# A deformable and a dynamic depthwise convolution: the chain of y in four steps, lag 19, taps two to a product, biases in one turn, pads ahead of the pivot

## The chip, the cores and the metric

The kernel runs on one core of one Trainium2 chip. The metric is the device time of one execution in microseconds; the median of the runs is given.

## The reference, cut to what matters

The input x is (8, 32, 192, 192) in fp32. Two stages, each preceded by a group norm of 16 groups of two channels, and each added to its input:

```python
def _L0(x, w_off, b_off, w_dcn, b_dcn):          # x: normalized
    off = (sigmoid(conv2d(x, w_off, b_off, 1)) - 0.5) * 2.0     # 3x3, 32 -> 64: dx, dy in (-1, 1)
    ix, iy = reflect(column - dx), reflect(row - dy)
    sampled = bilinear(x, iy, ix)                # per pixel and channel
    return conv2d(sampled, w_dcn, b_dcn, 1)      # 3x3, 32 -> 32

def _L1(y, w1, b1, w2, b2):                      # y: normalized
    hdn = relu(y.mean(axis=(2, 3)) @ w1 + b1)    # 64 per image
    kernels = (hdn @ w2 + b2).reshape(b, 32, 3, 3)
    return depthwise_conv3x3(y, kernels)         # own taps for each image and channel

y = x + _L0(group_norm(x), ...)
return y + _L1(group_norm(y), ...)
```

The taps of the second stage depend on the mean and the variance of the whole image y, so no row of the output can be made before the last row of y is there.

## The kernel before, in words

**Tiling.** An image is 12 chunks of 16 rows (CHUNKS), spread over 128 partitions; B = 8 images make TOTAL = 96 chunks. One loop of steps i runs on each engine, each writes its own order by hand, and semaphores tie them together; b, o = divmod(i, 12). In step i the engines work on these chunks:

- Chunk i: TensorE (PE) makes the offset convolution into the bank pair z (offsets, L357). ScalarE (ACT) takes its tanh, sign and size (offset, side, size) and copies neighbours (sides). VectorE (DVE) mixes the samples (sample, L699 to L727), nine instructions, the last at L727.
- Chunk i - 3 (DCN_STEP): PE's deformable convolution into dc in two halves (deform, L397 to L406). DVE adds bias and residual (evacuate, L739) and so has y in the ring yr of YS = 15 chunks; ACT sums its squares (y_square).
- Chunk i - 17 (DW_STEP): PE's depthwise convolution in two halves (depthwise, L427), into the one bank dw, each half emptied by ACT (finish, L575). For the last image the two banks dc are free and are used in turn. Steps 99 to 112 hold only this work.

PE's order in a step: offsets, first half of depthwise, first half of deform, second half of depthwise, second half of deform.

**Small work once an image.** All small products write columns of one bank sm and take turns in the order of small_order: PE waits until ACT has read the result before (small_turn). For the norm of y of image b - 1: y_totals on ACT at o = 3, y_means on PE at the end of o = 3, ACT reads it at o = 4, POOL computes the norm (y_norm, L856 to L868) and writes pads (set_y_pads), PE makes the hidden layer (hidden, L476) behind the offset products of o = 4 and the 16 taps (taps, L483) behind the first half of deform of the same step. In fp32 each product is two instructions. ACT reads the taps at o = 5, POOL makes the depthwise weights wy (y_weights) and PE their bias (y_bias, L493) at o = 5, where the depthwise of the image begins.

For the norm of the next x: SP loads its eight plane tiles at o = 0 to 7 (st_load), ACT sums each a step later (x_sums, L583 and L586), shifted by a pivot value, which POOL takes from the first tile (pivot, L770, at o = 0). x_mean, x_var and x_biases follow on PE at the ends of o = 9, 10 and 11. x_biases makes two groups of bias products (L444, L464) with a read of ACT between them.

**Pads.** set_pads(n) (L824, L830) writes the halo columns of chunk n's input, which PE's offset products and ACT's sides wait for. For the first chunk of an image it runs at o = 11 of the image before, behind x_weights; for the second and third at o = 0 behind pivot. set_s_pads, set_first_edge and set_last_edge do the same for the sampled rows. set_y_edges (POOL, four small DMAs at o = 4, two images later) writes the last row's halo in y.

**SP.** In step i it issues the store of chunk i - 18, the shifts of sampled rows (s_shift, behind sampled), the loads of chunk i + 2 (x_load), a plane tile, the residual rows of chunk i - 3, and the shift of y rows for chunk i - 15 (y_shift; for the first of an image i - 16, which waits for the pads of y).

Of the kernel before, what the change touches and what calls it, by code (L numbers as in the profile page):

```python
# [30 lines left out]
XS, SS, YS, HS = 3, 3, 15, 4  # L31
# [15 lines left out]
DW_STEP = 17  # L47
# [50 lines left out]
def small_order():  # L98

    order = [("xm", 0), ("xv", 0), ("ob", 0), ("db", 0)]  # L100
    for b in range(B + 1):
        if b:
            order += [("ym", b - 1), ("hid", b - 1), ("tap", b - 1), ("wb", b - 1)]
        if b + 1 < B:
            order += [("xm", b + 1), ("xv", b + 1), ("ob", b + 1), ("db", b + 1)]
    return {key: i for i, key in enumerate(order)}
# [5 lines left out]
def block_kernel(nc, x, planes, w_off, b_off, w_dcn, b_dcn, w1, b1, w2, b2, consts, xr, out):  # L112
    with ExitStack() as ctx:
# [17 lines left out]
        ypad = sb("ypad", [P, Q, PW])  # L131
# [9 lines left out]
        w1r = sb("w1r", [P, Q, HID])  # L141
        w2r = sb("w2r", [HID, TAPS, P])
        b2r = sb("b2r", [P, TAPS])
        b1c = sb("b1c", [HID, 1])
# [22 lines left out]
        hid = sb("hid", [HID, 1])  # L167
# [183 lines left out]
        def _(pe):  # L351
# [87 lines left out]
            def biases(what, b, col, sets, mean):  # L439
                small_turn(what, b)  # L440
                for at, weights in enumerate(sets):
                    for kx in range(3):
                        for m in halves:
                            last = nc.tensor.matmul(sm[m, col + at:col + at + 1], weights[:, kx, :], mean,  # L444
                                                    start=kx == 0, stop=kx == 2)
                last.then_inc(small, 1)

# [8 lines left out]
            def x_biases(b):  # L456
                pe.wait_ge(wo_ok, b + 1)
                biases("ob", b, C_OB, (wos[b % 2][:, 0], wos[b % 2][:, 1]), nmx[b % 2][:])
                pe.wait_ge(wd_ok, b + 1)
                small_turn("db", b)  # L460
                for q in range(Q):
                    for kx in range(3):
                        for g in range(G):
                            last = nc.tensor.matmul(sm[C * g:C * g + C, C_DB + q:C_DB + q + 1], wds[b % 2][:, kx, q],  # L464
                                                    nmx[b % 2][:], start=kx == 0, stop=kx == 2)
# [6 lines left out]
            def hidden(b):  # L472
                pe.wait_ge(y_step, Y_STEPS * b + 7)
                small_turn("hid", b)
                for q in range(Q):
                    last = nc.tensor.matmul(sm[0:HID, C_HID:C_HID + 1], w1r[:, q], pooled[:, q:q + 1],  # L476
# [3 lines left out]
            def taps(b):  # L480
                small_turn("tap", b)
                for t in range(TAPS):
                    last = nc.tensor.matmul(sm[:, C_TAP + t:C_TAP + t + 1], w2r[:, t, :], hid[:],  # L483
                                            start=True, stop=True)
# [17 lines left out]
            for i in range(STEPS):  # L502
# [5 lines left out]
                if 0 < b <= B and o == 4:  # L508
                    hidden(b - 1)
                if 0 < b <= B and o == 5:  # L510
# [5 lines left out]
                if 0 < b <= B and o == 4:  # L516
# [5 lines left out]
                if 0 < b <= B and o == 3:  # L522
                    y_means(b - 1)
                if b + 1 < B:
# [8 lines left out]
        def _(act):  # L533
# [86 lines left out]

            def off_bias(b):
# [4 lines left out]
                                     bias=bo[:, 1:2], scale=0.5).then_inc(small_rd, 1)  # L626
                act.wait_ge(small_rd, SMALL["ob", b] + 1)
                act.wait_ge(small, SMALL["db", b] + 1)
                nc.scalar.activation(db[b % 2][:, 0:1], sm[:, C_DB:C_DB + 1], ACT.Identity, bias=bd[:, 0:1])
                nc.scalar.activation(db[b % 2][:, 1:2], sm[:, C_DB + 1:C_DB + 2], ACT.Identity,  # L630
                                     bias=bd[:, 1:2]).then_inc(small_rd, 1)
# [17 lines left out]
            for i in range(STEPS):  # L649
# [8 lines left out]
                if 0 < b <= B and o == 5:  # L658
                    read("tap", b - 1, tapr[:], sm[:, C_TAP:C_TAP + TAPS])
# [18 lines left out]
                if 0 < b <= B and o == 4:  # L678
                    read("hid", b - 1, hid[:], sm[0:HID, C_HID:C_HID + 1], ACT.Relu, bias=b1c[:], scale=1.0 / (2 * G))
                if 0 < b <= B and o == 5:  # L680
# [10 lines left out]
        def _(dve):  # L691
# [38 lines left out]
            def evacuate(n):  # L730
# [3 lines left out]
                if j == 0:  # L734
                    dve.wait_ge(small_rd, SMALL["db", b] + 1)
# [8 lines left out]
            dve.wait_ge(cleared, 3)  # L744
# [16 lines left out]
        def _(pool):  # L761
# [83 lines left out]
            def set_last_edge(b):  # L845
                q = slice(P // 2, P)
                pool.wait_ge(dcn_mm, 2 * (CHUNKS * b + CHUNKS - SS))
                if b + 1 < B:
                    pool.wait_ge(pads, pads_set(CHUNKS * (b + 1)))
# [20 lines left out]
            def set_y_pads(b):  # L870
# [8 lines left out]
                wait(pool, e_in, 16 * EDGES * b)  # L879
# [140 lines left out]
```

## Time and profile before

| | |
|---|---|
| median of 3 runs | 1694.75 us (1694.44 to 1696.19) |
| profiled execution | 1700.7 us, its span 1698.9 us |
| PE busy | 1574.7 us, 93% |
| DVE busy | 1356.8 us, 80% |
| ACT busy | 1052.9 us, 62% |
| POOL busy | 313.5 us, 18% |
| mean granted clock of PE | 0.967 |
| hardware DMA queue | 304 MB, 60.5% of 16 engines |

All times of the trace are microseconds from the start of the span. A busy PE is not a PE at its peak: records of products overlap. The granted clock is the share of PE's full rate (1.00 is 2.4 GHz, 0.50 is 1.2). "Idle before" and the bracket behind an instruction say how long its engine did nothing and what ended that.

### The profile page before, as it was taken

The numbers are of one execution on the slowest core, as the hardware profiler recorded it, in microseconds if no ns is written. First come the engines' busy times: TensorE is split into PE (matmuls) and PEld (weight loads), VectorE is DVE, ScalarE is ACT, GpSimd is POOL, SyncE is SP. The second block draws the span as 40 slices with busy tenths as digits, with TensorE's granted clock in tenths as the row PEclk, the third lists the DMA queues.
The fourth block names the chain that finished last, engine by engine and source line by source line (L and its number), as shares of the span: only waits on it lengthen the run. The fifth ranks groups of instructions, "written<-read, shape, count | busy, mean of one in ns | idle before, by whom it ended". The sixth has DMA issues, their size and how long they took to land.

```text
span 1698.9 us, 30216 instructions
## 1 busy us (share of the span) xinstructions
PE 1574.7 (93%) x12176; PEld 671.1 (40%) x12176; DVE 1356.8 (80%) x1264; ACT 1052.9 (62%) x1586; POOL 313.5 (18%) x381
## 2 busy tenths in 40 slices
PE   3779878999999999999999999999999999999887
PEld 1333334333443334433443334433444334533343
DVE  3899989798879978799887987798787898889700
ACT  4766556765777566666667656676575765655413
POOL 3000312012230221203230122301403031300010
PEclk9899999999999999999999999999999999999979
DMA  7355446666666665666666666666565765556436
GB/s 231 107 178 169 140 124 198 174 200 202 191 210 196 173 205 169 193 203 195 184 207 184 199 198 179 194 197 191 168 213 171 220 171 164 177 158 193 132 89 199
DMA packets 225195, 307.73 MB, mean 181 GB/s; under 512 B 16656, under 2 KB 167552, under 8 KB 224992
## 3 DMA queue, kind: packets, MB, share of 16 engines
q1 hardware_dynamic: 223632, 304.42, 60.5%
q8 instruction: 96, 1.57, 0.4%
q0 software_dynamic: 1424, 1.38, 0.3%
q14 instruction: 43, 0.35, 0.1%
HBM read 190.11 MB, written 38.14 MB: 134 GB/s over the span
## 4 chain that ended last, share of the span: by engine, by line
PE 54%; DVE 19%; ACT 11%; issue 6%; DMA 5%; POOL 3%; SPq 2%; DVEq 0%; ACTq 0%; POOLq 0%
PE z L357 25%; PE dc L397 13%; PE dw L427 9%; DMA st<-in_planes 4%; DVE nb L718 3%; DVE nb L713 3%; DVE nb L716 3%; PE sm L483 2%; ACT dv L540 2%; PE dc L427 2%; DVE xv L706 2%; DVE nb L720 2%; DVE nb L722 2%; ACT mv L547 2%; DVE nb L707 2%
## 5 line engine op out<-in xcount | busy, mean ns | idle before, releaser
L357 PE MATMUL z<-xv,wos 128*64 128x384 f32 x4608 | 775.5, 493 | 33.9 <-issue 22.6
L357 PEld LDWEIGHTS z<-xv,wos 128*64 128x64 f32 x4608 | 333.6, 137 | 454.0 <-issue 445.8
L397 PE MATMUL dc<-sr,wds 128*32 128x384 f32 x2304 | 453.4, 525 | 25.7 <-DVE yr L739 25.6
L397 PE MATMUL dc<-sh,wds 128*32 128x384 f32 x2112 | 411.8, 527 | 0.0
L699 DVE COPY_PREDICATED nb<-mu,xv 128x2280 f32<-128x2280 uint16 x96 | 268.8, 2800 | 100.0 <-ACT mu L547 99.1
L427 PE MATMUL dw<-yr,wy 128*64 128x388 f32 x672 | 258.1, 506 | 4.6 <-ACT ot L575 3.7
L427 PE MATMUL dw<-yh,wy 128*64 128x388 f32 x672 | 258.2, 506 | 0.0
L540 ACT ACTIVATE du<-z,ob 128x768 f32<-128x768 f32 x96 | 86.3, 899 | 275.2 <-PE z L357 275.2
L397 PEld LDWEIGHTS dc<-sr,wds 128*32 128x32 f32 x2304 | 123.4, 111 | 296.4 <-issue 294.8
L561 ACT ACTIVATE nb<-xv 128x2292 f32<-128x2292 f32 x96 | 202.7, 2112 | 41.7 <-issue 41.3
L706 DVE COPY_PREDICATED xv<-mv,xv 128x768 f32<-128x768 uint16 x96 | 102.5, 1067 | 90.6 <-ACT mv L547 67.7
L718 DVE TENSOR_TENSOR nb<-nb,xv 128x1536 f32<-128x1536 f32 x96 | 169.6, 1767 | 3.3
L716 DVE TENSOR_TENSOR nb<-nb,du 128x1536 f32<-128x1536 f32 x96 | 169.0, 1760 | 3.3
L713 DVE TENSOR_TENSOR nb<-nb,xv 128x1536 f32<-128x1536 f32 x96 | 169.0, 1760 | 3.3
L427 PEld LDWEIGHTS dw<-yr,wy 128*64 128x64 f32 x672 | 84.1, 137 | 139.9 <-issue 87.2
L575 ACT ACTIVATE ot<-dw,wb 128x388 f32<-128x388 f32 x168 | 96.7, 576 | 68.8 <-PE dw L427 68.4
L594 ACT ACTIVATE junk<-yr,nmx 128x768 bf16<-128x768 f32 x96 | 89.4, 932 | 66.3 <-DVE yr L739 66.0
L739 DVE SCALAR_TENSOR_TENSOR yr<-dc,db,yr 128x384 f32<-128x384 f32 x192 | 110.6, 613 | 21.5 <-PE dc L406 9.1
L727 DVE TENSOR_TENSOR sr<-nb 128x768 f32<-128x768 f32 x96 | 93.1, 969 | 32.4 <-PE dc L397 20.8
L583 ACT ACTIVATE st<-st,npiv 128x1152 f32<-128x1152 f32 x56 | 70.1, 1253 | 75.4 <-DMA st<-in_planes 75.4
L397 PEld LDWEIGHTS dc<-sh,wds 128*32 128x32 f32 x2112 | 113.2, 112 | 0.8 <-issue 0.8
L707 DVE COPY_PREDICATED nb<-mv,nb 128x768 f32<-128x768 uint16 x96 | 100.4, 1046 | 0.0
(118 smaller groups left out, 1619.4 us busy)
## 6 DMA issues: line engine op xcount, KB each, us to landing
xv<-in_x SPq DMA_DIRECT2D x272, 384.0 KB, 4.7
yr<-in_xr SPq DMA_DIRECT2D x96, 392.0 KB, 7.7
out<-ot SPq DMA_DIRECT2D x96, 388.0 KB, 3.7
yh<-yr SPq DMA_DIRECT2D x179, 196.0 KB, 6.8
st<-in_planes SPq DMA_DIRECT2D x56, 576.0 KB, 7.1
sh<-sr SPq DMA_DIRECT2D x160, 194.0 KB, 2.8
sh<-sr SPq DMA_DIRECT2D x32, 145.5 KB, 2.5
yr<-in_planes SPq DMA_DIRECT2D x8, 576.0 KB, 12.0
```

What stands on the lines that cost most here:

```text
L357: last = nc.tensor.matmul(acc[m], weights[:, kx, :], view[:, :, kx:kx + W], start=kx == 0, stop=kx == 2)
L397: last = nc.tensor.matmul(dc[m, q, 0:NB * PAIRS], weights[:, kx, q], view[:, :, cols], start=first, stop=final)
L427: last = nc.tensor.matmul(acc[m], wy[b % 2][:, q, t], view[:, :, t:t + OW], start=t == 0, stop=t == 1)
L540: nc.scalar.activation(d[:].rearrange("p (h k) w -> p h (k w)", h=2), z[:, i, :, 0:HALF * W], ACT.Tanh, bias=ob[b % 2][:, i:i + 1], scale= ...
L561: nc.scalar.activation(nb[s][:, :, :, 1:W], v[:, :, :, 1:W], ACT.Copy)
L699: nc.vector.copy_predicated(q[:, :, :, 1:W - 1], m3[:, :, :, 1:W - 1], v[:, :, :, 3:W + 1]).then_inc(lerp, 1)
L706: nc.vector.copy_predicated(v[:, ABOVE, :, 1:W + 1], m1, v[:, BELOW, :, 1:W + 1]).then_inc(lerp, 1)
L707: nc.vector.copy_predicated(q[:, ABOVE], m1, q[:, BELOW]).then_inc(lerp, 1)
L713: nc.vector.tensor_tensor(two, two, own, ALU.subtract).then_inc(lerp, 1)
L716: nc.vector.tensor_tensor(two, two, u2, ALU.mult).then_inc(lerp, 1)
L718: nc.vector.tensor_tensor(two, two, own, ALU.add).then_inc(x_free, 1)
L739: nc.vector.scalar_tensor_tensor(out=y, in0=dc[:, q, 0:NB * PAIRS].rearrange("p (k w) -> p k w", w=PAIRS), scalar=db[b % 2][:, q:q + 1], i ...
```

## The change

DW_STEP grows from 17 to 19 and the ring of y from 15 to 17 chunks. The chain of the norm of y is spread: the hidden layer's products go to the end of step 4, ACT reads them at the head of step 5, the taps are made in step 5 and read at the head of step 6, POOL makes wy in step 6 and PE the bias in step 7. The hidden layer is made twice, in both halves of the partitions; ACT writes it as two columns of a 128x2 tile whose other halves are zero, and the weights of two taps are stacked in the rows, so eight products give the 16 taps. All bias products of x are one turn with one read. POOL sets the pads of an image's first two chunks at o = 11 of the image before and those of the third at o = 0 ahead of all else; pivot comes behind set_s_pads. set_y_edges moves to o = 5, behind the pads of the next y, and ypad has two buffers.

The diff, cut to its core:

```diff
@@ -28,7 +28,7 @@
...
-XS, SS, YS, HS = 3, 3, 15, 4
+XS, SS, YS, HS = 3, 3, 17, 4
@@ -44,7 +44,7 @@
...
-DW_STEP = 17
+DW_STEP = 19
@@ -97,12 +97,12 @@
...
-    order = [("xm", 0), ("xv", 0), ("ob", 0), ("db", 0)]
+    order = [("xm", 0), ("xv", 0), ("ob", 0)]
...
-            order += [("xm", b + 1), ("xv", b + 1), ("ob", b + 1), ("db", b + 1)]
+            order += [("xm", b + 1), ("xv", b + 1), ("ob", b + 1)]
@@ -128,7 +128,7 @@
...
-        ypad = sb("ypad", [P, Q, PW])
+        ypad = [sb(f"ypad{s}", [P, Q, PW]) for s in range(2)]
...
-        w1r = sb("w1r", [P, Q, HID])
-        w2r = sb("w2r", [HID, TAPS, P])
+        w1r = sb("w1r", [P, Q, P])
+        w2r = sb("w2r", [P, TAPS // 2, P])
...
-        b1c = sb("b1c", [HID, 1])
+        b1c = sb("b1c", [P, 1])
...
-        hid = sb("hid", [HID, 1])
+        hid = sb("hid", [P, 2])
@@ -455,14 +446,19 @@
...
             def x_biases(b):
                 pe.wait_ge(wo_ok, b + 1)
-                biases("ob", b, C_OB, (wos[b % 2][:, 0], wos[b % 2][:, 1]), nmx[b % 2][:])
                 pe.wait_ge(wd_ok, b + 1)
-                small_turn("db", b)
+                small_turn("ob", b)
+                mean = nmx[b % 2][:]
+                for i in range(2):
+                    for kx in range(3):
+                        for m in halves:
+                            nc.tensor.matmul(sm[m, C_OB + i:C_OB + i + 1], wos[b % 2][:, i, kx], mean,
+                                             start=kx == 0, stop=kx == 2)
                 for q in range(Q):
                     for kx in range(3):
                         for g in range(G):
                             last = nc.tensor.matmul(sm[C * g:C * g + C, C_DB + q:C_DB + q + 1], wds[b % 2][:, kx, q],
-                                                    nmx[b % 2][:], start=kx == 0, stop=kx == 2)
+                                                    mean, start=kx == 0, stop=kx == 2)
                 last.then_inc(small, 1)
@@ -473,14 +469,14 @@
...
-                    last = nc.tensor.matmul(sm[0:HID, C_HID:C_HID + 1], w1r[:, q], pooled[:, q:q + 1],
+                    last = nc.tensor.matmul(sm[:, C_HID:C_HID + 1], w1r[:, q], pooled[:, q:q + 1],
...
             def taps(b):
                 small_turn("tap", b)
-                for t in range(TAPS):
-                    last = nc.tensor.matmul(sm[:, C_TAP + t:C_TAP + t + 1], w2r[:, t, :], hid[:],
+                for t in range(TAPS // 2):
+                    last = nc.tensor.matmul(sm[:, C_TAP + t:C_TAP + TAPS:TAPS // 2], w2r[:, t, :], hid[:],
                                             start=True, stop=True)
                 last.then_inc(small, 1)
@@ -505,15 +501,13 @@
...
-                if 0 < b <= B and o == 4:
-                    hidden(b - 1)
-                if 0 < b <= B and o == 5:
+                if 0 < b <= B and o == 7:
                     y_bias(b - 1)
                 if c >= 0:
                     depthwise(c, 0)
                 if 0 <= d < TOTAL:
                     deform(d, 0)
-                if 0 < b <= B and o == 4:
+                if 0 < b <= B and o == 5:
                     taps(b - 1)
                 if c >= 0:
                     depthwise(c, 1)
@@ -521,6 +515,8 @@
                     deform(d, 1)
                 if 0 < b <= B and o == 3:
                     y_means(b - 1)
+                if 0 < b <= B and o == 4:
+                    hidden(b - 1)
@@ -618,17 +614,24 @@
...
+            def hidden_read(b):
+                act.wait_ge(small, SMALL["hid", b] + 1)
+                for half_of, m in enumerate((slice(0, HID), slice(HID, P))):
+                    last = nc.scalar.activation(hid[m, half_of:half_of + 1], sm[m, C_HID:C_HID + 1], ACT.Relu,
+                                                bias=b1c[m], scale=1.0 / (2 * G))
+                last.then_inc(small_rd, 1)
...
             def off_bias(b):
...
-                                     bias=bo[:, 1:2], scale=0.5).then_inc(small_rd, 1)
+                                     bias=bo[:, 1:2], scale=0.5)
+                for q in range(Q):
+                    last = nc.scalar.activation(db[b % 2][:, q:q + 1], sm[:, C_DB + q:C_DB + q + 1], ACT.Identity,
+                                                bias=bd[:, q:q + 1])
+                last.then_inc(small_rd, 1)
                 act.wait_ge(small_rd, SMALL["ob", b] + 1)
-                act.wait_ge(small, SMALL["db", b] + 1)
-                nc.scalar.activation(db[b % 2][:, 0:1], sm[:, C_DB:C_DB + 1], ACT.Identity, bias=bd[:, 0:1])
-                nc.scalar.activation(db[b % 2][:, 1:2], sm[:, C_DB + 1:C_DB + 2], ACT.Identity,
-                                     bias=bd[:, 1:2]).then_inc(small_rd, 1)
@@ -656,6 +659,8 @@
...
                 if 0 < b <= B and o == 5:
+                    hidden_read(b - 1)
+                if 0 < b <= B and o == 6:
                     read("tap", b - 1, tapr[:], sm[:, C_TAP:C_TAP + TAPS])
@@ -675,9 +680,8 @@
...
-                if 0 < b <= B and o == 4:
-                    read("hid", b - 1, hid[:], sm[0:HID, C_HID:C_HID + 1], ACT.Relu, bias=b1c[:], scale=1.0 / (2 * G))
-                if 0 < b <= B and o == 5:
+                if 0 < b <= B and o == 7:
+                    wait(act, o_done, Q * CHUNKS * (b - 1))
                     read("wb", b - 1, wb[:], sm[:, C_WB:C_WB + Q], bias=mvy[:, 0:1])
                     act.wait_ge(small_rd, SMALL["wb", b - 1] + 1)
@@ -846,7 +850,7 @@
...
                 if b + 1 < B:
-                    pool.wait_ge(pads, pads_set(CHUNKS * (b + 1)))
+                    pool.wait_ge(pads, pads_set(CHUNKS * (b + 1) + 2))
@@ -876,8 +880,8 @@
...
-                wait(pool, e_in, 16 * EDGES * b)
-                ts(ypad[:].rearrange("p q w -> p (q w)"), zero[:, 0:Q * PW], mvy[:, 0:1], None,
+                wait(pool, e_in, 16 * EDGES * (b - 1))
+                ts(ypad[b % 2][:].rearrange("p q w -> p (q w)"), zero[:, 0:Q * PW], mvy[:, 0:1], None,
@@ -921,22 +926,24 @@
             for i in range(STEPS):
                 b, o = divmod(i, CHUNKS)
+                if b < B and o == 0:
+                    if b == 0:
+                        set_pads(i + 1)
+                    set_pads(i + 2)
                 if 0 < b <= B and o == 0:
                     set_last_edge(b - 1)
                 if b < B and o == 0:
-                    if b + 1 < B:
-                        pivot(b + 1)
-                    set_pads(i + 1)
-                    set_pads(i + 2)
                     set_first_edge(b)
                 if b < B and o < SS:
                     set_s_pads(i)
-                if b >= 2 and o == 4:
-                    set_y_edges(b - 2)
+                if b + 1 < B and o == 0:
+                    pivot(b + 1)
                 if 0 < b <= B and o == 4:
                     y_norm(b - 1)
                     set_y_pads(b - 1)
-                if 0 < b <= B and o == 5:
+                if b >= 2 and o == 5:
+                    set_y_edges(b - 2)
+                if 0 < b <= B and o == 6:
                     y_weights(b - 1)
                 if b < B and o == 6:
                     edge_weights(b)
@@ -947,8 +954,9 @@
...
                 if b + 1 < B and o == 11:
+                    set_pads(i + 1)
                     x_weights(b + 1)
-                    set_pads(i + 1)
+                    set_pads(i + 2)
...
-    w2 = np.zeros((HID, TAPS, P), chan_w2.dtype)
+    w2 = np.zeros((2, HID, TAPS // 2, P), chan_w2.dtype)
-        w2[:, at, on] = chan_w2[:, c[on], ky[on], kx[on]]
+        w2[q, :, at % (TAPS // 2), on] = chan_w2[:, c[on], ky[on], kx[on]].T
```

## Rows read from the trace of the kernel before

**Rows 1.** The page, busy time: us, share of the span, instructions.

```profile
PE 1574.7 (93%) x12176; PEld 671.1 (40%) x12176; DVE 1356.8 (80%) x1264; ACT 1052.9 (62%) x1586; POOL 313.5 (18%) x381
```

**Rows 2.** Timeline of DVE (start, us, instruction); then the chain that ended last.

```profile
140.93 0.96 DVE L727 TENSOR_TENSOR sr<-nb 128x768 f32<-128x768 f32 x1
170.96 0.96 DVE L727 TENSOR_TENSOR sr<-nb 128x768 f32<-128x768 f32 x1
...
315.74 7.89 PE z L357 x48
...
345.86 7.89 PE z L357 x48
```

**Rows 3.** Stretches: us, busy (instructions) by engine, clock, DMA share, GB/s.

```profile
1205.62:1240.33 34.71, 31.94 (x224) 13.80 (x224) 26.24 (x26) 21.39 (x32) 8.23 (x7) 0.95 0.64 188
sum 171.32, PE 156.57 PEld 67.61 DVE 131.07 ACT 109.56 POOL 39.50; mean PE 31.31 PEld 13.52 DVE 26.21 ACT 21.91 POOL 7.90
...
1407.02:1437.29 30.27, 30.22 (x225) 12.36 (x225) 25.93 (x26) 18.76 (x27) 5.11 (x6) 1.00 0.56 161
```

**Rows 4.** Timeline of POOL and PE at the seam of image 4.

```profile
819.27 0.56 POOL L770 TENSOR_SCALAR npiv<-st 128x1 f32<-128x1 f32 x1 [14.37 <-DMA st<-in_planes]
...
823.60 0.86 PE L357 MATMUL z<-xv,wos 128*64 128x384 f32 x4 [2.70 <-issue]
```

**Rows 5.** Timeline of DVE, chunks 12, 13, 15 and 17.

```profile
232.49 0.96 DVE L727 TENSOR_TENSOR sr<-nb 128x768 f32<-128x768 f32 x1
252.44 0.96 DVE L727 TENSOR_TENSOR sr<-nb 128x768 f32<-128x768 f32 x1
...
283.42 0.96 DVE L727 TENSOR_TENSOR sr<-nb 128x768 f32<-128x768 f32 x1
...
319.49 0.96 DVE L727 TENSOR_TENSOR sr<-nb 128x768 f32<-128x768 f32 x1
```

**Rows 6.** Stretches from chunk 12b+4 to 12b+6, first of six, and their sum.

```profile
475.48:511.38 35.90, 34.68 (x277) 15.97 (x277) 28.52 (x28) 23.84 (x37) 13.18 (x17) 1.00 0.67 202
...
sum 226.69, PE 220.63 PEld 100.94 DVE 170.57 ACT 138.04 POOL 86.66; mean PE 36.77 PEld 16.82 DVE 28.43 ACT 23.01 POOL 14.44
```

**Rows 7.** Waits: engine, line, waited for, us in total, times, longest.

```profile
PE sm L476 <- POOL pooled L867: 15.5, 7, 6.6
PE sm L464 <- ACT ob L625: 5.2, 8, 1.0
```

**Rows 8.** Chain (taps, bias of y); weight loads of the averages; a stretch, image 7.

```profile
488.64 3.66 PE sm L483 x32
...
308.10 0.41 PE sm L493 x15
...
L436 PEld LDWEIGHTS sm<-xn,kc 128*128 128x128 f32 x32 | 5.2, 203 | 34.6 <-issue 33.1 <-POOL xn L789 1.5
...
1487.50:1490.00 2.50, 2.50 (x18) 0.68 (x20) 2.43 (x3) 0.66 (x2) 1.07 (x2) 0.50 0.67 211
```

**Rows 9.** The chain that ended last, in the tail.

```profile
1633.52 0.59 ACT ot L575
...
1639.10 6.92 PE sm L483 x32
...
1652.32 17.42 PE dc L427 x88
```

**Rows 10.** Chain and DVE's timeline around a plane tile; DMA issues, us to landing.

```profile
530.69 0.97 DVE sr L727
...
535.42 8.37 DMA st<-in_planes
...
561.47 0.96 DVE L727 TENSOR_TENSOR sr<-nb 128x768 f32<-128x768 f32 x1
...
st<-in_planes SPq DMA_DIRECT2D x56, 576.0 KB, 7.1
...
yr<-in_planes SPq DMA_DIRECT2D x8, 576.0 KB, 12.0
```

More of the change, by code:

```diff
@@ L437, in average @@
                     .then_inc(small, 1)
[L439 to L446, printed above, removed]
             def x_mean(b):
@@ L734, in evacuate @@
                 if j == 0:
-                    dve.wait_ge(small_rd, SMALL["db", b] + 1)
+                    dve.wait_ge(small_rd, SMALL["ob", b] + 1)
                 for q in range(Q):
@@ L742, in evacuate @@
                         accum_out=ys1[b % 2][:, q, j:j + 1]).then_inc(y_done, 1)
-            dve.wait_ge(cleared, 3)
+            dve.wait_ge(cleared, 4)
             dve.wait_ge(piv, 1)
@@ L888, in set_y_edges @@
                 for p0 in (P - 3 * CQ, P - CQ):
-                    pool.dma_start(yr[p0:p0 + CQ, k], ypad[p0:p0 + CQ]).then_inc(e_in, 16)
+                    pool.dma_start(yr[p0:p0 + CQ, k], ypad[b % 2][p0:p0 + CQ]).then_inc(e_in, 16)
                 for p0 in (0, C):
-                    pool.dma_start(yh[p0:p0 + CQ, h], ypad[p0:p0 + CQ]).then_inc(e_in, 16)
+                    pool.dma_start(yh[p0:p0 + CQ, h], ypad[b % 2][p0:p0 + CQ]).then_inc(e_in, 16)
             def y_weights(b):
@@ L910, in _ @@
             nc.gpsimd.memset(wde[:], 0.0).then_inc(cleared, 1)
+            nc.gpsimd.memset(hid[:], 0.0).then_inc(cleared, 1)
             for t, a in ((kc, consts), (wo, w_off), (bo, b_off), (wd, w_dcn), (bd, b_dcn), (w1r, w1),
@@ L913, in _ @@
                 pool.dma_start(t[:], a).then_inc(loaded, 16)
-            pool.wait_ge(cleared, 3)
+            pool.wait_ge(cleared, 4)
             pivot(0)
@@ L1004 @@
         "b_dcn": asc(asc(L0_conv_b_dcn).reshape(CQ, Q)[pc]),
-        "w1": asc(asc(L1_conv_w1).reshape(CQ, Q, HID)[pc]),
-        "b1": asc(L1_conv_b1).reshape(HID, 1),
-        "w2": w2,
+        "w1": asc(np.tile(asc(L1_conv_w1).reshape(CQ, Q, HID)[pc], (1, 1, 2))),
+        "b1": asc(np.tile(asc(L1_conv_b1), 2)).reshape(P, 1),
+        "w2": w2.reshape(P, TAPS // 2, P),
         "b2": b2,
```

## The prediction, on record before the changed kernel ran

> **What bounds the kernel now.** First the page: TensorE (PE) is busy for 93% of the span [rows 1]. A share says little about a loop of 96 equal steps, so next come the starts of one instruction in successive steps. Before any depthwise work exists, DVE's last instruction of a chunk comes at 140.93 and two steps later at 170.96: 15.02 us a step, set by DVE and ACT, since PE lacks the depthwise products then. Once they are there, the offset products start at 315.74 and two steps later at 345.86: 15.06 us a step, back to back on PE [rows 2]. The two loops are equal, so a plain step can't become faster by taking work off one of them. Yet the image from 1205.62 to 1407.02 takes 201.4 us, 16.8 for each of its 12 steps [rows 3]. The excess over 15.06 is what is to be had, and it stands at the image's seams.
>
> **Pads ahead of the pivot.** At o = 0 POOL first runs pivot, whose input, the first plane tile of the next image, is there only at 819.27, after 14.37 us of waiting; the pad writes stand behind it, and the products of chunk 49 start at 823.60 after 2.70 us in which PE waited for nothing else [rows 4]. The stretch from the first products of chunk 12b to those of 12b+2 takes 171.32 us in sum for b = 2 to 6. For b = 7 there is no pivot, and it takes 30.27 [rows 3]: nearly the experiment itself. 171.32 - 5 x 30.27 = 20.0 us goes. Part of it is clock: the last of the five has a granted clock of 0.95, that of b = 7 has 1.00. For b = 1 PE is not the bound, but DVE is held up too: chunk 13 ends 19.95 us after chunk 12 instead of 15.02 [rows 5], so 4.9 us goes. What is new on POOL: the pivot stands behind set_s_pads, which waits for the second deform of step 12b, that is for PE's last work ahead of the products of the next step (820.9 in the example, 823.60 less 2.70). Behind the pivot waits ACT's first plane sum, and behind that the tanh of the step, which can't start before the first half of the offset products is done, 4 us into the step. Pivot to 821.6 and two passes of ACT over the tile, an estimated 2.8 us, make 824.4, against 824.9: it just fits. The pads of chunk 12b go ahead of x_weights at o = 11, where POOL waits most of a step for the variance; those of 12b+2 need only products that are over: nothing. Bounds: 0 (the stall comes back behind the pivot) and 24.9; I take 24.9, by the row of b = 7.
>
> **The chain of y over four steps.** The stretch from the first products of chunk 12b+4 to those of 12b+6 takes 226.69 us in sum for b = 2 to 7, 37.8 each, for two steps of 15.06 [rows 6]. What fills it: the wait of the hidden layer for POOL's pooled means (15.5 us in all, the longest 6.6 in image 1, the other six 1.5 each) [rows 7], the tap products, the bias of y, and a half clock behind the taps [rows 8]. After the change the hidden layer's products stand behind the step's depthwise and deform halves, 15.06 - 7.89 = 7.2 us later: no wait, 0.4 us of PE. The taps are 32 instructions in 3.66 us, 0.114 each; 16 now, 1.83 us. That they cost the same with 128 rows of weights and two columns, I take from the averages, whose 128x128 weights load in 203 ns [rows 8], less than two of the taps' turns; bounds 1.83 and 3.66. So two steps take 2 x 15.06 + 0.4 + 1.83 = 32.35, six images 194.1, and 32.6 goes. The bias of y moves to step 7 and costs its 0.41 us there, six times: 30.2 left. This has the clock whole. In image 7, which has no such wait, it fell to 0.50 (1.2 GHz) behind the taps with PE busy 2.50 of 2.50 us [rows 8]: what came before the fall was the run of tap products. That half the run leaves it whole is a guess; no row shows it, and rival A holds the other way.
> The Trainium skill (TensorE: Matmul & The Clock Gate, HAM oscillation) puts such falls down to idle gaps of PE. By that rule the removed waits would cure them and A could not be, with the same sum; the row of image 7 is against it.
> For b = 1 DVE takes 36.07 us for the two steps from 283.42 to 319.49; PE has time to spare there, and they become 30.03: 6.0 us goes [rows 5]. The edges at o = 5 are issued by POOL behind set_y_pads and behind the shift of the image's last chunk, which SP issues at o = 4; the depthwise that reads them comes at o = 6. SP's own wait for the pads of y is gone as well. Hidden, and free as long as POOL is less than a step late.
>
> **Lag 19.** PE does no less than before. Steps 17 and 18 lose their depthwise, but DVE holds them at 15.02, so nothing is won, and two chunks move to the tail. The two more slots of yr keep the residual loads as early as they are.
>
> **Biases in one turn.** ACT's read between the two groups of products is gone: PE waited for it 5.2 us in 8 turns [rows 7], about 1.0 of it at the seam of image 1, where DVE is the bound. 4.2 us goes; z follows directly, so nothing hid it. ACT's four reads are together as long as before.
>
> **The tail.** Chunk 82 leaves its bank at 1633.52, one chunk is left, and the chain of y is bare: means, taps at half clock (6.92 us instead of 3.66), POOL, and the last image's products start at 1652.3; 88 of them take 17.42 us, 3.1 more than 44 pairs at 0.325 (the 1.30 us of a half at full clock), since the clock is still low at first [rows 9]. After the change the chunk at this place is 80. Six halves follow on one bank, each 1.5 us of PE and 0.6 of ACT with their signals, 2.2 in turn: 1634.1 + 13.2, plus 1.2 of the taps that ACT's reads don't cover and 0.6 for the bias: 1649.1. So 3.2 us earlier, and 3 more if the clock stays whole; a little goes back, as the shifts of the next chunks are then just in time: 5 us. Bounds: -3 (it falls as before, while six halves run) and 7.
>
> **What the faster pace costs.** A plane tile is requested two DVE chunks ahead. One chunk ends at 530.69, the tile asked for behind it takes 8.37 us to land, and the next but one ends at 561.47: 15.39 a step, 0.33 over the plain one [rows 10]. With the pauses gone more steps may run by this loop, none or all 56 that have tiles: 0 to 18 us. The median landing is 7.1, with which the loop is 14.8 and doesn't bind, so I take 12 of the 56: 4 us.
>
> **Sum.** 24.9 + 6.0 + 30.2 + 4.2 + 5 - 4 = 66.3 us. The profiled execution took 1700.7 us (span 1698.9): 1634.4. The median of the runs is 6 below it, 1694.75: 1628.5, and I say 1629.
>
> **Rivals.**
> A. The clock still falls behind the taps. For: it fell once without any wait ahead. Against: half the run of small products, with full ones on both sides. Its price is what six stretches have over the undisturbed first, 226.69 - 6 x 35.90 = 11.3 us: 1640. Chance 15%.
> B. The pad stall turns into a wait on the pivot. For: 0.5 us of margin, and POOL is slow while DVE works. Against: it must be late by more than that in each image. Two us late is 1.5 x 5 = 8 us: 1637; the whole stall back is 1654. Chance 12%.
> C. The loop through the plane tile takes over: all 56 steps 0.33 slower, 18 us instead of 4: 1643. For: the faster pace presses the same transfers together. Against: the median of 7.1. Chance 15%.
> D. Slower than before: the same loop with the landing L longer still. The loop is (30.78 - 8.37 + L)/2. It decides from where 56 steps eat the 70 us that the other terms give, 1.25 each: a step of 16.31, L = 10.2 us. Tiles that queued eight deep at the start took 12.0 [rows 10]; at that L a step takes 17.2, 120 us more, 50 over what is won: 1745. Against: it would take this queue in every step. Chance 3%.
> E. Moved turns held up on ACT: a read at the head of a step (hidden layer, taps) that comes late holds the tanh. 1 us in 7 images: 1636. Chance 5%.
> The forecast itself has 50%, with 1620 to 1637.
>
> **Numbers.** The range is 1614 to 1647. Its lower end has the tail at 7, no cost of pace and 9 us more, should small gaps of ACT and PE close too; its upper end takes in A, C and most of B. What a measurement tells from no change is about 0.2%, 3.4 us. Faster 0.96 (all but D and what nobody listed), same 0.01, slower 0.03.
>
> **What would show it.** No wait of PE ahead of the products of chunk 12b+1, and 30.3 us from 12b to 12b+2 in every image. 16 tap products an image in 1.8 us, the clock 1.00 behind them, 32.4 us from 12b+4 to 12b+6. DVE at 15.02 in steps 13, 16 and 17. An image between 188 and 191 us. The last image's depthwise from 1649 - 61 = 1588 on. Wrong would be: images above 193 us, a median landing of plane tiles near 10 us, or a pivot that ends over 1 us behind the step's last deform.

## The result, and the profile after

The changed kernel took 1631.64 us in the median of 4 runs (1628.14 to 1634.07) beside 1694.6 us (1690.29 to 1696.19) of the kernel before on the same chip: a ratio of 0.9631 [0.9604, 0.9658]. The forecast was 1629, range 1614 to 1647. The profiled execution took 1630.0 us, its span 1628.2, its mean granted clock 0.986: against the profiled execution of before the span is 70.7 us shorter, some 8 more than the medians say, since that execution was 6 above the median and this one 1.6 below.

The page of the kernel after, busy time (it answers to [rows 1]) and two DMA rows:

```profile
PE 1535.3 (94%) x12048; PEld 644.3 (40%) x12048; DVE 1359.2 (83%) x1264; ACT 1053.2 (65%) x1594; POOL 326.2 (20%) x382
...
st<-in_planes SPq DMA_DIRECT2D x56, 576.0 KB, 7.1
...
yr<-in_planes SPq DMA_DIRECT2D x8, 576.0 KB, 10.3
```

PE lost 39 us of busy time for 128 instructions fewer. At 0.114 us each [rows 8] these are 14.6 of it; an estimate puts most of the other 25 down to products that no longer run at half clock, since the mean granted clock rose from 0.967 to 0.986. DVE and ACT are busy for as long as before.

The stretches from chunk 12b to 12b+2, the first and the last of the five, and their sum (they answer to [rows 3]):

```profile
395.71:426.17 30.46, 30.34 (x226) 12.29 (x225) 26.88 (x26) 21.46 (x33) 4.18 (x3) 1.00 0.64 188
...
1156.29:1186.70 30.41, 30.26 (x224) 12.41 (x224) 26.70 (x26) 21.45 (x33) 4.04 (x3) 1.00 0.64 186
...
sum 152.18, PE 151.36 PEld 61.70 DVE 134.06 ACT 107.26 POOL 20.70; mean PE 30.27 PEld 12.34 DVE 26.81 ACT 21.45 POOL 4.14
```

Each is 30.4 us with PE busy for 30.3 of it and the clock whole: the seam costs nearly what a plain pair of steps costs, 30.1. The timeline of POOL, PE, DVE and ACT at the seam of image 4 says why (it answers to [rows 4]):

```profile
791.29 0.76 POOL L842 TENSOR_SCALAR sr<-zero,mx 128x8 f32<-128x8 f32 x1 [13.55 <-PE dc L397]
792.13 1.62 POOL L774 TENSOR_SCALAR npiv<-st 128x1 f32<-128x1 f32 x1
...
791.11 7.96 PE L357 MATMUL z<-xv,wos 128*64 128x384 f32 x48
...
791.90 1.76 DVE L722 TENSOR_TENSOR nb<-nb,xv 128x1536 f32<-128x1536 f32 x1
...
796.38 0.88 ACT L536 ACTIVATE du<-z,ob 128x768 f32<-128x768 f32 x1
...
798.24 2.79 DVE L703 COPY_PREDICATED nb<-mu,xv 128x2280 f32<-128x2280 uint16 x1 [0.43 <-ACT mu L543]
```

The products of chunk 49 start at 791.11, straight behind the last deform products. POOL does its s pads when PE's deform is over, and the pivot behind them has its tile already: nothing in brackets. But the pivot takes 1.62 us here and ends at 793.75, 0.09 us behind the end of DVE's sum at 793.66 and 2.6 behind the deform. ACT's two passes over the tile follow, and the tanh starts at 796.38, 5.3 us into the step. DVE waits 0.43 us for what comes of it.

The stretches from 12b+4 to 12b+6, first and last of six, and their sum (they answer to [rows 6]):

```profile
459.75:492.36 32.61, 32.61 (x246) 13.93 (x245) 29.98 (x28) 23.71 (x36) 14.61 (x15) 1.00 0.65 199
...
1409.98:1442.58 32.60, 32.60 (x245) 13.93 (x244) 29.84 (x28) 18.80 (x28) 14.90 (x15) 1.00 0.55 161
...
sum 195.60, PE 195.60 PEld 83.82 DVE 178.35 ACT 137.44 POOL 83.58; mean PE 32.60 PEld 13.97 DVE 29.73 ACT 22.91 POOL 13.93
```

PE is busy 32.61 of 32.61 us at full clock. The taps in the chain, their weight loads in the lines by form, and what ACT and PE wait for (they answer to [rows 7, 8]):

```profile
486.90 1.88 PE sm L479 x16
```
```profile
L479 PEld LDWEIGHTS sm<-hid,w2r 128*128 128x128 f32 x128 | 14.9, 191 | 5.4 <-issue 5.4
```
```profile
ACT st L579 <- DMA st<-in_planes: 98.6, 38, 8.0
ACT st L579 <- POOL npiv L774: 22.2, 6, 3.9
PE z L357 <- ACT du L536: 10.9, 2, 10.0
PE dw L427 <- ACT ot L571: 9.2, 9, 3.1
```

No wait for the pooled means is left. The tail, in the chain that ended last (it answers to [rows 9]):

```profile
1576.61 1.88 PE sm L479 x16
1578.49 1.48 PE dw L427 x8
...
1585.34 16.21 PE dc L427 x96
...
1615.45 3.86 issue
1619.31 5.45 PE dc L427 x16
```

### The profile page after: what moved, and what is told of

Read it like the earlier page. It is cut to its first block, busy times and chain, and to the rows that moved or that the text cites. A ratio compares the mean times of both kernels' runs of the same rounds, so it can differ in the third digit from the quotient of the medians.

```text
span 1628.2 us, 29952 instructions
## 1 busy us (share of the span) xinstructions
PE 1535.3 (94%) x12048; PEld 644.3 (40%) x12048; DVE 1359.2 (83%) x1264; ACT 1053.2 (65%) x1594; POOL 326.2 (20%) x382
## 4 chain that ended last, share of the span: by engine, by line
PE 65%; DVE 14%; ACT 9%; DMA 4%; issue 4%; SPq 2%; POOL 1%; DVEq 0%; ACTq 0%; POOLq 0%
PE z L357 31%; PE dc L397 16%; PE dw L427 11%; DMA st<-in_planes 3%; DVE nb L722 2%; DVE nb L720 2%; DVE nb L717 2%; ACT dv L536 2%; PE dc L427 2%; ACT mv L543 1%; DVE xv L710 1%; PE dc L401 1%; DVE nb L724 1%; DVE nb L726 1%; DVE nb L711 1%
## 5 line engine op out<-in xcount | busy, mean ns | idle before, releaser
L357 PE MATMUL z<-xv,wos 128*64 128x384 f32 x4608 | 769.2, 490 | 11.1 <-ACT du L536 10.9
L357 PEld LDWEIGHTS z<-xv,wos 128*64 128x64 f32 x4608 | 327.9, 137 | 425.7 <-issue 414.4
L397 PE MATMUL dc<-sr,wds 128*32 128x384 f32 x2304 | 448.2, 520 | 35.8 <-DVE yr L743 35.7
L397 PE MATMUL dc<-sh,wds 128*32 128x384 f32 x2112 | 406.7, 521 | 0.0
L427 PE MATMUL dw<-yr,wy 128*64 128x388 f32 x672 | 252.4, 497 | 11.6 <-ACT ot L571 9.2
L427 PE MATMUL dw<-yh,wy 128*64 128x388 f32 x672 | 252.5, 497 | 0.0
L579 ACT ACTIVATE st<-st,npiv 128x1152 f32<-128x1152 f32 x56 | 70.3, 1256 | 120.8 <-DMA st<-in_planes 98.6
L590 ACT ACTIVATE junk<-yr,nmx 128x768 bf16<-128x768 f32 x96 | 89.4, 931 | 66.3 <-DVE yr L743 66.0
## 6 DMA issues: line engine op xcount, KB each, us to landing
yr<-in_planes SPq DMA_DIRECT2D x8, 576.0 KB, 10.3
```

The source lines that it names most:

```text
L357: last = nc.tensor.matmul(acc[m], weights[:, kx, :], view[:, :, kx:kx + W], start=kx == 0, stop=kx == 2)
L397: last = nc.tensor.matmul(dc[m, q, 0:NB * PAIRS], weights[:, kx, q], view[:, :, cols], start=first, stop=final)
L427: last = nc.tensor.matmul(acc[m], wy[b % 2][:, q, t], view[:, :, t:t + OW], start=t == 0, stop=t == 1)
```

## The experiments

All were run with five rounds, in three groups, each with the kernel before on the same chip: its median was 1695.9, 1697.07 and 1698.96 us. "+" is slower than what the kernel is an edit of, by medians within the group where there is one.

**The kernel after once more.** 

> The changed kernel once more, as the yardstick for the three runs beside it: 0.963 of the kernel before, 1628 to 1635 us. No theory turns on it.

1630.88, ratio 0.9617 [0.9595, 0.9639]. In the third group: 

> The changed kernel itself, as the yardstick for the three runs beside it: 0.962 of the kernel before. No theory turns on it.

1631.64, ratio 0.9608 [0.9584, 0.9632]. The three intervals overlap, so edits of a few us can be told against it.

**Old order of pads and pivot.** In the kernel after, POOL's turns at o = 0 and 11 as before:

```diff
+                    if b + 1 < B:
+                        pivot(b + 1)
+                    set_pads(i + 1)
+                    set_pads(i + 2)
                     set_first_edge(b)
```

> The changed kernel with pivot and pads in the order of before (pivot first, pads of an image's second and third chunk behind it at o = 0). Theory: the stall at the seam is worth what the stretches from chunk 12b to 12b+2 had over 30.3, so 20 to 25 us come back, 1652 to 1656; PE waits 2.7 us or more ahead of the products of chunk 12b+1 for b = 1 to 6, with a granted clock below 1 behind the longer ones. Rival: PE and DVE make up for the pause within the image and the gain came from the chain of y: under 8 us.

1660.34, ratio 0.9790: +29, above the expected 20 to 25. Its stretches from 12b to 12b+2 (b = 2, and the sum), its wait at the offset products, and the timeline of POOL at the seam of image 4:

```profile
398.91:433.00 34.09, 30.36 (x225) 13.16 (x225) 26.68 (x26) 21.45 (x33) 7.49 (x7) 1.00 0.64 184
...
sum 175.40, PE 157.67 PEld 66.57 DVE 134.95 ACT 112.41 POOL 37.80; mean PE 31.53 PEld 13.31 DVE 26.99 ACT 22.48 POOL 7.56
```
```profile
PE z L357 <- issue: 26.2, 6, 8.6
```
```profile
800.66 0.32 POOL L774 TENSOR_SCALAR npiv<-st 128x1 f32<-128x1 f32 x1 [13.97 <-DMA st<-in_planes]
800.96 5.68 POOL L834 TENSOR_SCALAR xv<-zero,mx 128x8 f32<-128x8 f32 x4
```

The stall is back as in [rows 3, 4]: the pads take 5.68 us behind a pivot that waited for its tile. The sum is 23.2 over that of after, and chunk 13 of image 1 ends 5.0 later behind chunk 12. Up to the last chunk the two profiles differ by 24.2, so some 4 are won back in other steps. The profiled execution is the shortest of its five, 5.7 below their median, which is the rest. In four of the five stretches the granted clock is 0.95: it falls where PE stands idle for 2.7 to 3.7 us at the seam.

**Sixteen taps in 32 instructions of 64 rows.** In the kernel after, the weights not stacked, the rest as it is:

```diff
-                for t in range(TAPS // 2):
-                    last = nc.tensor.matmul(sm[:, C_TAP + t:C_TAP + TAPS:TAPS // 2], w2r[:, t, :], hid[:],
+                for t in range(TAPS):
+                    last = nc.tensor.matmul(sm[:, C_TAP + t:C_TAP + t + 1], w2r[:, t, :], hid[:],
```

> The changed kernel with 16 tap products of 64 rows and one column instead of 8 of 128 rows and two, the chain still over four steps. Theory: 16 more instructions at 0.114 us in each of 8 images, 1.8 us each in steps where PE is the bound, 11 to 15 us in all with the clock whole, 1643 to 1646; and, if the run of tap products is what brings the clock down, it falls to 0.50 behind them in most images although no wait is ahead of them, and the price is 20 to 27 us. Rival: the fall came from the wait for the pooled means, so the clock stays 1.00 and the price is 11 us at most.

1654.26, ratio 0.9745: +23 (its profiled execution is the longest of its six, 13 above the median, so the rows overstate it). Stretches from 12b+4 to 12b+6, first and sum, and then, around the taps of the first, which start at 491.6:

```profile
464.88:502.09 37.21, 37.21 (x261) 18.76 (x261) 32.01 (x30) 24.89 (x39) 14.31 (x15) 0.91 0.58 178
...
sum 223.24, PE 223.24 PEld 112.86 DVE 192.38 ACT 141.36 POOL 84.51; mean PE 37.21 PEld 18.81 DVE 32.06 ACT 23.56 POOL 14.09
```
```profile
488.00:491.50 3.50, 3.50 (x34) 1.29 (x30) 2.52 (x3) 3.39 (x6) 0.00 (x0) 1.00 0.97 281
491.50:496.00 4.50, 4.50 (x38) 4.39 (x34) 4.39 (x4) 1.84 (x2) 0.00 (x0) 0.83 0.78 283
496.00:500.00 4.00, 4.00 (x17) 1.12 (x20) 3.33 (x3) 1.14 (x2) 0.00 (x0) 0.50 0.00 0
```

PE is busy in every microsecond of these stretches, and no wait stands ahead, yet the clock is at 1.00 before the taps, at 0.50 (1.2 GHz) behind them, in all six images. It falls while the taps run, 2.4 to 3.1 us behind their start. A stretch costs 4.6 us over that of after; sixteen more instructions at the rate of [rows 8] are 1.8 of it, and what is left, 2.8, is the clock. In this execution the clock is thus more than half of what stacking gives in a stretch. By the medians it is less: sixteen more instructions in six stretches and in the tail are an estimated 12.8 of the 23 us, and some 10 are left for the clock. The six executions had mean clocks from 0.967 (the profiled one) to 0.981 (the fastest, 1646.57).

**Two turns for the biases of x.** In the kernel after:

```diff
-                pe.wait_ge(wd_ok, b + 1)
                 small_turn("ob", b)
...
+                last.then_inc(small, 1)
+                pe.wait_ge(wd_ok, b + 1)
+                small_turn("db", b)
```

> The changed kernel with the bias products in two turns, ACT's read between them. Theory: PE waits 0.6 us between them at each seam where it is the bound, 4 us slower in all, 1635 to 1637. Rival: z's start is set by something else by now (ACT or DVE), and nothing changes.

1633.31, ratio 0.9636: +2.4. The ratios' intervals overlap with those of after, but all four runs (1633.25 to 1636.55) lie above all four of after in this group (1629.45 to 1632.58), so the sign is as expected. PE's wait is back as in [rows 7]:

```profile
PE sm L462 <- ACT ob L630: 5.2, 8, 1.0
```

DVE's first step of images 2 to 7 takes 17.2 us again instead of 16.5, 4 us in sum; in the medians 2.4 of it show.

**Lag 19 alone.** In the kernel before, lag, ring, ypad and the place of set_y_edges; in it the bias of y is read while two chunks of the image before are still to be finished. These two chunks get the next image's bias, which changes their values and none of the work:

```diff
-XS, SS, YS, HS = 3, 3, 15, 4
+XS, SS, YS, HS = 3, 3, 17, 4
...
-DW_STEP = 17
+DW_STEP = 19
```

> The kernel before with lag 19 and a ring of 17 chunks alone (the edges of y at o = 5 with two buffers of ypad, as the lag asks for); chain, taps, biases and pads as before. Theory: PE's work stays the same and the two chunks moved out of steps 17 and 18 are added behind the chain of the last image, where each half costs 2.2 us on its one bank: 5 to 9 us slower than before, 1701 to 1705. Rival: two more chunks cover the bare chain of the last image, 3 to 6 us faster.

1707.92, ratio 1.0069 [1.0044, 1.0093]: +10.9, slower than the expected 5 to 9. In the profile DVE's last sampling instruction starts at 1601.39, in before at 1602.13, and the tail behind it takes 102.9 us instead of 96.8. By itself the lag only costs. The spread chain needs a longer lag than 17, since the depthwise weights come a step later and their bias two; whether 18 would do was not tried, nor was the spread without the lag.

**Stacked taps alone.** In the kernel before, the taps, the hidden layer and its read as in the change.

```diff
-        w2r = sb("w2r", [HID, TAPS, P])
+        w2r = sb("w2r", [P, TAPS // 2, P])
```

> The kernel before with the taps stacked two to a product alone; the hidden layer still waits for the pooled means at the head of o = 4. Theory: half the run of tap products, 1.8 us less in 6 images, and no fall of the clock behind them (11 us of falls before), a few us in the tail: 22 to 28 us faster than before, 1668 to 1674, the clock 1.00 in the stretches from chunk 12b+4 to 12b+6, which take 34.1 us. Rival: the wait ahead of the hidden layer brings the clock down, as the rule on idle gaps has it; the falls stay and the gain is 11 to 14 us.

1670.89, ratio 0.9855: -26. Stretches from 12b+4 to 12b+6 (first, sum), its wait for the means, and then those from 12b to 12b+2 (b = 4, sum):

```profile
473.73:508.18 34.45, 33.22 (x261) 14.36 (x260) 28.59 (x28) 24.07 (x38) 13.44 (x17) 1.00 0.72 210
...
sum 205.24, PE 199.13 PEld 85.89 DVE 170.50 ACT 139.67 POOL 86.15; mean PE 33.19 PEld 14.32 DVE 28.42 ACT 23.28 POOL 14.36
```
```profile
PE sm L476 <- POOL pooled L874: 15.6, 7, 6.7
```
```profile
799.40:836.10 36.70, 32.91 (x224) 13.64 (x224) 26.37 (x26) 22.78 (x34) 7.08 (x7) 0.91 0.61 180
...
sum 180.43, PE 162.57 PEld 68.42 DVE 131.86 ACT 113.94 POOL 38.19; mean PE 32.51 PEld 13.68 DVE 26.37 ACT 22.79 POOL 7.64
```

The wait is as long as before [rows 7]: 1.2 us in images 2 to 6, which ends 4 us ahead of the taps. The clock stays at 1.00. The first sum falls by 21.5. The second is 9.1 over [rows 3], with a clock of 0.91 to 0.95 and PE idle at the seam for 3.7 us in four of five images, where it was 2.7 in four of five. The old order above, also with stacked taps, has 3.7 us in four of five too, and the lag alone, without them, in one of five. So stacking may lengthen this stall; no run shows why, and this execution is the longest of its six, 8 above their median.

**The chain not spread.** In the kernel after, hidden layer and taps both in step 4, as in before, wy in step 5; lag and stacking stay:

```diff
-                if 0 < b <= B and o == 5:
+                if 0 < b <= B and o == 4:
                     taps(b - 1)
```

> The changed kernel with the chain drawn together again: hidden layer and taps both at o = 4 (products of the hidden layer ahead of the depthwise, as before), POOL's weights at o = 5; lag, stacked taps, biases and pads stay as changed. Theory: the wait for the pooled means comes back, 1.2 us in five images, none in image 7, little in image 1, and the clock stays whole behind the stacked taps; with the bare chain in the tail that is 8 to 14 us slower than the changed kernel, 1639 to 1645. Rival: it is the spread that took most of the 30 us at the chain, 20 us or more come back.

1649.88, ratio 0.9719: +18.2, above the expected 8 to 14 and below the rival's 20. The stretches from 12b+4 to 12b+6 (first, sum), the wait, and the tail behind its taps:

```profile
467.06:501.03 33.97, 32.73 (x246) 13.83 (x245) 28.05 (x27) 23.68 (x37) 17.00 (x21) 1.00 0.61 190
...
sum 202.65, PE 196.49 PEld 83.14 DVE 168.41 ACT 138.09 POOL 102.39; mean PE 32.75 PEld 13.86 DVE 28.07 ACT 23.01 POOL 17.06
```
```profile
PE sm L472 <- POOL pooled L871: 15.9, 7, 6.9
```
```profile
1590.00:1594.00 4.00, 4.00 (x20) 3.79 (x20) 0.00 (x0) 0.59 (x1) 1.52 (x4) 0.50 0.06 13
1594.00:1598.00 4.00, 3.22 (x11) 0.84 (x9) 0.00 (x0) 0.66 (x2) 0.56 (x2) 0.50 0.00 0
...
1610.00:1614.00 4.00, 4.00 (x36) 2.19 (x34) 0.00 (x0) 1.44 (x3) 0.00 (x0) 0.77 0.54 162
```

Up to the last chunk it is 14.2 us over after: 6.7 in image 1, 7.1 in the six stretches. The tail is 11.2 longer in this execution (the runs are in two bunches, 1649 to 1650 and near 1655; this is of the second). In the tail the clock falls at 1588.0, 2.2 us ahead of the taps, behind waits of PE of 1.7 and 2.9 us. The cover of the chain by PE's other work is thus worth most where there is little else: in image 1 and in the tail.

**The plane tile first in SP's step.** In the kernel after (what is taken out stood behind x_load):

```diff
                 b, o = divmod(i, CHUNKS)
+                if b + 1 < B and o < STILES:
+                    st_load(b + 1, o)
                 if 0 <= i - DW_STEP - 1:
                     store(i - DW_STEP - 1)
```

> The changed kernel with SP's load of the plane tile at the head of its step, ahead of the store and of the shifts that wait for sampled, instead of behind them: the tile is asked for some 8 us earlier. Theory: the loop through the tile is what makes step 8 of an image 15.5 to 16.7 us and holds the pivot at o = 0; without it 1 us in each of 7 images, 1622 to 1626, ACT's wait for tiles falls from 99 us to under 30 (images 1 to 7 nearly none). Rival: PE sets the pace there and the wait lies in ACT's slack: the same time within 2 us.

1626.02, ratio 0.9584 [0.9556, 0.9611]. In the third group: 

> The changed kernel with the plane tile asked for at the head of SP's step, again, beside the changed kernel on one chip. Theory: 3 to 6 us faster than it, 0.3%, from step 8 of some images and the seams. Rival: the difference seen in separate calls was one of chips, under 2 us here.

1627.83, ratio 0.9584 [0.9561, 0.9606], beside 1631.64 of after: 3.8 us, with four of its five runs below all five of after. ACT waits for no plane tile any more, only for the pivot:

```profile
ACT st L579 <- POOL npiv L774: 20.4, 6, 3.9
```
```profile
st<-in_planes SPq DMA_DIRECT2D x56, 576.0 KB, 8.4
```

The landing takes longer than in after and costs nothing, since it starts earlier. The theory named step 8 and the seams. In the two profiles the time from the end of the first image to the last sample is 2 us shorter than in the three of after (1322.1 and 1322.0 instead of 1324.1, 1324.2 and 1323.6), nearly all of it in step 8; the rest is in the first image, which ends at 212.0 and 211.4 instead of 214.2, 215.7 and 214.3. This is the best version found: it beats both kernels.

**The plane tile last in SP's step**, behind the shift of y, which waits for DVE and for PE's depthwise:

```diff
                         y_shift(n)
+                if b + 1 < B and o < STILES:
+                    st_load(b + 1, o)
```

> The changed kernel with SP's load of the plane tile at the end of its step, behind the residual and the shift of y: it is asked for 2 to 3 us later. Theory (the loop through the tile is the next bound): half of the delay, 1 to 1.5 us, in up to 56 steps, 40 to 80 us slower than the changed kernel, 1670 to 1710. Rival: slack of ACT and the buffers takes most of it, under 15 us slower.

1667.15, ratio 0.9820: +36 over after (measured in the other groups), 41 over the tile first. That is under the expected 40 to 80 and over the rival's 15. Its waits:

```profile
ACT st L579 <- DMA st<-in_planes: 199.3, 47, 8.4
...
PE dw L427 <- ACT ot L571: 36.3, 24, 6.8
```
```profile
st<-in_planes SPq DMA_DIRECT2D x56, 576.0 KB, 8.5
```

With the landing of the kernel that asks first, 8.5 us beside 8.4, the place of the request alone decides: ACT, in order, waits for the tile, and PE for the bank that ACT would have emptied behind it. That is the loop of rivals C and D, which hardly binds in the kernel after.

**The plane tile first, in the kernel before**, the same move. 

> The kernel before with nothing changed but the place of SP's load of the plane tile: at the head of its step. Theory: the pivot's 14 us of waiting for its tile is what holds the pads at the seam, so the tile asked for earlier removes most of that stall by the other end, 18 to 27 us faster than before, 1668 to 1678, and PE's wait ahead of the products of chunk 12b+1 is gone or under 1 us. Rival: POOL's order itself (four slow pad writes at o = 0) holds PE, and the gain is under 8 us.

1664.17, ratio 0.9800: -34.8, more than the expected 18 to 27. Stretches from 12b to 12b+2 (b = 4, sum), and its pivots' waits:

```profile
789.72:819.97 30.25, 30.19 (x226) 12.23 (x225) 26.03 (x26) 22.36 (x33) 3.92 (x7) 1.00 0.68 187
...
sum 151.31, PE 151.04 PEld 61.61 DVE 129.98 ACT 111.86 POOL 19.30; mean PE 30.21 PEld 12.32 DVE 26.00 ACT 22.37 POOL 3.86
```
```profile
POOL npiv L770 <- DMA st<-in_planes: 18.5, 6, 4.3
```

With the pads still behind the pivot, the seam is as short as in after: the tile comes before POOL needs it. Pads ahead of the pivot and the tile ahead in the queue cure one and the same stall. What the expectation left out is beside the seam: by the profiles DVE's step 8 takes 3.5 us less over seven images, the first image 3.4 less, and step 4, where the clock can fall behind the taps, 5.0 less.

## Why the prediction was right, step by step

The sum of the terms was 66.3 us; the span lost 70.7 and the medians 63. The stated 1629 was reached by taking off the 6 us by which the profiled execution of before lay above its median; that of after lay 1.6 below its own. So part of the closeness of 1629 to 1631.64 is luck. Two steps failed, and both were small: the cost of the pace, and the time at which the pivot ends.

- **Pads** (24.9): 171.32 to 152.18 is 19.1 of the 20.0; chunk 13 of image 1 ends 15.05 behind chunk 12 instead of 19.95, the 4.9 forecast. Undoing it costs 24.2 by the profile and 29 by the medians. But the pivot doesn't just fit. It was put at 0.7 us behind the step's last deform and called wrong beyond 1; in images 2 to 6 it ends 2.6 behind it in each, because it takes 1.62 us and not the 0.56 of [rows 4]. That time isn't its own: in all these profiles it ends 0.09 us or a little more behind the end of the DVE sum beside which it began. The tanh starts 5.3 us into the step, 1.3 later than the products allow. So what rival B needs did happen, and its price did not: DVE waits 0.43 us and its step is 15.2 instead of 15.0, where B had 1.5 us an image. So the forecast was right here by slack of DVE that it didn't count, and not by its margin of 0.5 us.
- **Chain of y** (30.2 and 6.0): the stretches lost 31.1 (226.69 to 195.60). The bias of y in step 7 takes 0.45 an image, 2.7, where 0.41 was put: 28.4. Steps 16 and 17 of image 1 lost 5.8. The taps take 1.88 us where 1.83 was forecast, and a stretch is 32.6 where 32.35 was.
- **The clock behind the taps**, called a guess: right. It is 1.00 in all six stretches, and rival A falls. The two kernels that have one half each show which half of the change cures it: 32 tap instructions with no wait ahead lose it in six of six images (unstacked), 16 with a wait of 1.2 us ahead keep it (stacked alone, not spread). Over all profiles of this study, images 2 to 7, the clock falls during or within 1.5 us behind 20 of 24 runs of 32 taps (it stays whole in the first stretch of [rows 6]) and 1 of 60 runs of 16. That one is in the kernel with the tile last, where PE then waited for ACT:

```profile
1082.49 1.95 PE L479 MATMUL sm<-hid,w2r 128*128 128x2 f32 x16
1085.60 0.91 PE L427 MATMUL dw<-yr,wy 128*64 128x388 f32 x1 [1.16 <-ACT ot L571]
```

The Trainium skill (TensorE: Matmul & The Clock Gate, HAM oscillation) puts such falls down to idle gaps of PE. At the seams and in the tail these runs agree: with the old pivot the clock falls in four of five stretches where PE stands idle for 2.7 to 3.7 us, and in after, where it doesn't, in none; in the kernel not spread it falls behind the waits of the tail. Behind the taps they don't: in the unstacked kernel it fell with PE busy throughout. What about the run of small products does it (their one column, their idle rows, the weight loads, 4.39 of 4.50 us in that row) was not taken apart.
- **Biases** (4.2): DVE's step 12b is 16.5 instead of 17.3, 0.74 at each of the six seams from image 2 on and nothing in image 1, 4.4 us; undone, 4 by the profile and 2.4 by the medians.
- **Lag 19**: next to nothing in the body, as forecast (the last sample at 1601.39 and 1602.13); in the tail 6.1 by the profile, and 10.9 in all by the medians, part of the next term.
- **The tail** (5, bounds -3 and 7): 96.8 to 90.0 us behind the last sample, 6.8. The last image's depthwise starts at 1585.34 where 1588 was forecast, and the clock was whole behind its taps: the case of "3 more if the clock stays whole". The two other profiles of after have tails of 90.8 and 91.9. In the kernel with the chain not spread the clock falls there, and the tail takes 101.2.
- **Pace** (-4): the step that failed is the count of steps that come to run by the tile loop, 12 of 56. The kernels with the tile first say what the loop costs in step 8, summed over seven images: 3.5 us already in before and 2.3 in after (4.3 and 2.1 in its two other profiles). So the faster pace added nothing that shows. ACT's waits for tiles did grow, from 75.4 to 98.6 us, but ACT has this time to spare. The loop is real, and its length isn't the landing but the landing and the place of the request in SP's order, which the prediction didn't weigh: 8.5 us at the last place cost 36 us over 7.1 at the old place, and at the first place 8.4 takes 4 less than the old one does.
- **Not in the sum**: the first image ends at 214.19 instead of 216.99, with the first tiles landing in 10.3 us instead of 12.0. The profiles of this study have it between 211.4 and 217.0. The three with the tile first are the lowest; the three of after spread by 1.5, so part of it belongs to the execution. Images 2 to 7 take 188.9 to 190.5 us, inside the forecast 188 to 191. And two readings were loose: the waits for the means of "the other six 1.5 each" are 1.2 in images 2 to 6, none in 7 and 2.8 in the tail, and "two us late is 1.5 x 5 = 8 us" is 7.5.

Taken out of after one at a time, the parts are worth 29 (pads), 23 (stacking), 18 (spreading) and 2 (biases), and the lag, put into before, costs 11: 61 in sum, against 63 to 67 measured in the groups. That they add so well is not a given: the tile first is worth 35 us in before and 4 in after, since it and the pads cure one stall.

Two things stay open: what it is about the run of small products that the clock reacts to, and whether the seam costs more with the taps stacked.

## What to carry to other kernels

Take the forecast of a stall from the same loop's undisturbed copy (here image 7, which has no pivot): it was within 0.2 us a stretch. In an engine or a queue that works in order, the place of an instruction is a cost of its own: one DMA request cost 36 us at a later place and gave back 4 at an earlier one, landing in 8.5 and 8.4 us. In the kernel before, the earlier place gave 35. Pack small fp32 products into few instructions with all rows in use; they cost their own time and, in long runs, the clock of the full products behind them.

## What the runs showed of the hardware that was not expected

- A weight load of 128 rows and 128 columns took 191 ns, one of 64 rows and 128 columns 224 in before and 216 unstacked (where part of the time is at half clock). At full clock the whole instruction took 0.117 us with 128 rows and 0.114 with 64: filling the idle rows cost next to nothing. A load of 128 rows and 64 columns took 136 to 152.
- PE's granted clock went from 1.00 to 0.50 with PE busy 100% of the time, 2.4 to 3.1 us into a run of 32 one-column products (unstacked), and the records of the deform products behind it are 0.85 us long instead of 0.52. Half of such a run left it at 1.00 in 59 of 60 cases.
- The pivot, one value for each of 128 partitions, took 0.24 us beside an idle DVE (at 33.45 in before) and 0.24 to 1.82 us beside one of DVE's float32 sums of two inputs. In all 70 cases of images 2 to 6 in the fourteen profiles it began during such a sum; in 65 it ended 0.09 us behind the sum's end, in the other five it took its 0.24 us and ended 0.12 to 0.24 behind it. In the kernel after this makes it 1.62 us in each of these images. That POOL's access is held back by DVE's sum is argued from these rows; no run moved the two apart.
